# A two-layer graph network on one core: the first layer's gathered chunks as three-part 16-bit rows

## The reference, cut to what matters

```python
# 12500 nodes x 32 values; 212500 edges, sorted by dst
# layer 0: sum of scaled neighbour rows
norm = deg_inv_sqrt[row] * deg_inv_sqrt[col]
msgs = embedding_weight[row] * norm[:, None]
out = jax.ops.segment_sum(msgs, col, num_segments=n)
x = _layernorm(x + out, axis=-1)
# layer 1: an edge network makes 4 x 8 x 8 weights per edge, messages are summed by dst
x = _layernorm(x + _L1_gnn_ref(x, ...), axis=-1)
```

## Time and profile before

| | |
|---|---|
| median of 3 runs | 3307.98 us (3302.31 to 3311.62) |
| the profiled execution | 3305.82 us, its span 3304.0 us |
| layer 0's counted and gathered stage | from about 80 to 1182 us of the span |
| PE / DVE / ACT / POOL busy over the span | 79% / 87% / 38% / 72% |
| chain that ended last, by engine | POOL 31%, PE 22%, DVE 22%, issue 14%, ACT 10% |

### The profile page before, as it was taken

The page is one execution under the profiler, slowest core; times in us unless marked ns, Lnnn a source line. Parts: engine busy times, 40 slices in busy tenths (PEclk is TensorE's granted clock), DMA queues, the critical chain, the costliest instruction groups (busy, mean ns, idle before and its releaser), DMA issues.

```text
span 3304.0 us, 49643 instructions
## 1 busy us (share of the span) xinstructions
PE 2608.2 (79%) x17448; PEld 1564.6 (47%) x17534; DVE 2882.3 (87%) x5078; ACT 1267.8 (38%) x1963; POOL 2386.6 (72%) x2477
## 2 busy tenths in 40 slices
PE   5799999999989967777777777777777777777776
PEld 4567676766667743333333333333343333333333
DVE  7777877777777749999999999999999999999998
ACT  2787878887878741111111111111111111111111
POOL 1777777777767747777777777777777777777775
PEclk6899999999999988998888989988888888988897
DMA  3000000000000021111111111111111111111112
GB/s 79 13 14 14 14 14 14 14 13 14 14 13 14 14 35 32 28 28 28 28 28 28 28 32 29 28 28 28 28 28 29 31 28 29 28 28 28 28 32 37
DMA packets 169352, 84.63 MB, mean 26 GB/s; under 512 B 112473, under 2 KB 155289, under 8 KB 169113
## 3 DMA queue, kind: packets, MB, share of 16 engines
q0 software_dynamic: 78336, 40.26, 8.2%
q1 hardware_dynamic: 90777, 41.20, 5.3%
HBM read 76.48 MB, written 4.81 MB: 25 GB/s over the span
## 4 chain that ended last, share of the span: by engine, by line
POOL 31%; PE 22%; DVE 22%; issue 14%; ACT 10%; DMA 1%; DVEq 1%; POOLq 0%; SPq 0%; ACTq 0%
POOL xg L551 31%; PE ps L813 10%; ACT room L619 9%; DVE stage L1514 7%; PE ps L828 5%; DVE prod_all L1504 4%; PE ps L753 3%; DVE prod_all L1498 3%; DVE oh L1190 1%; DVE prod_all L1324 1%; DVE stage L1488 1%; PE ps L800 1%; DVE stage L1484 1%; PE ps L721 1%; DVE lane L1322 1%
## 5 line engine op out<-in xcount | busy, mean ns | idle before, releaser
L551 POOL DMA_INDIRECT xg<-x_table,idx x1664 | 1572.6, 945 | 545.4 <-issue 501.6
L551 POOL DMA_INDIRECT xg<-scaled_x_table,efT_all x784 | 801.4, 1022 | 285.7 <-issue 226.0
L619 ACT ACTIVATE room<-ps 128x1089 bf16<-128x1089 f32 x800 | 880.3, 1205 | 204.9 <-PE ps L813 204.5
L936 PE MATMUL ps<-w2t,hT 128*128 128x512 f32 x1664 | 883.7, 657 | 18.1 <-ACT hT L670 17.9
L1514 DVE TENSOR_REDUCE stage<-prod_all 128x192 f32<-128x1536 f32 x416 | 725.4, 1744 | 3.2
L813 PE MATMUL ps<-prod_all,lane 128*128 128x363 bf16 x2640 | 560.8, 321 | 111.1 <-ACT room L619 64.4
L936 PEld LDWEIGHTS ps<-w2t,hT 128*128 128x128 f32 x1664 | 346.7, 214 | 377.3 <-issue 248.0
L828 PE MATMUL ps<-stage,room 128*128 128x96 bf16 x7840 | 465.6, 207 | 0.0
L670 ACT ACTIVATE hT<-ps,b 128x512 f32<-128x512 f32 x208 | 142.9, 687 | 830.1 <-PE ps L924 830.0
L924 PE MATMUL ps<-efT_all,w 128*128 128x512 f32 x416 | 266.5, 727 | 244.6 <-DMA sh<-in_sh 244.2
L828 PEld LDWEIGHTS ps<-stage,room 128*128 128x128 bf16 x7840 | 418.5, 98 | 84.4 <-issue 1.7
(11 more groups left out here) (155 smaller groups left out, 1627.5 us busy)
## 6 DMA issues: line engine op xcount, KB each, us to landing
efT_all<-in_efT SPq DMA_DIRECT2D x104, 256.0 KB
xg<-x_table,idx POOLq DMA_INDIRECT x1664, 2.4
xg<-scaled_x_table,efT_all POOLq DMA_INDIRECT x784
sh<-in_sh SPq DMA_DIRECT2D x104, 32.0 KB
idx<-in_src SPq DMA_DIRECT2D x104, 8.0 KB, 1.6
scaled_x_table<-room SPq DMA_DIRECT2D x2, 784.0 KB, 3.4
x_table<-x_sb SPq DMA_DIRECT2D x7, 224.0 KB, 4.4
out_rows<-room SPq DMA_DIRECT2D x6, 224.0 KB
```

Source lines behind the costliest of these rows:

```text
L551: pool.indirect_dma_start(to, None, table, bass.IndirectOffsetOnAxis(ap=at, axis=0)).then_inc(landed, 16)
L619: act.activation(counts[u % 2][:, :, t * TWIN:(t + 1) * TWIN].rearrange("p (r h) w -> p r h w", r=RANGES), ps_ring[i % 2].rearrange("p r ( ...
L936: mm = pe.matmul(ps_bank[j % 2][v], hT[j // 2][:, t * P:(t + 1) * P], w2t[:].rearrange("p h c o i -> p (h c o i)"), start=False, stop=True)
```

## The change

From the third chunk on (n >= 2), a chunk's rows come from a second DRAM table, `split_d`, a copy of the three-part 16-bit table that SP writes once `low_part` is done. Each gather then brings 128 rows of 96 16-bit values (192 bytes for 128 before). The masks of these chunks are written as 16-bit values, PE sums them by 16-bit products with 96 stationary columns, and DVE adds 96 partitions in place of 32. The first two chunks stay as they were. The buffers move into one SBUF tensor, `gathered`, and share space; DVE's wait for the remapped indices moves ahead of the first chunk's masks, since their place now holds what the remapping reads. The other branch (graphs whose edges are not near) joins the parts on DVE and does not run here.

```diff
+        split_d = nc.dram_tensor("split_table", (NPAD, D3), BF16).ap()
...
-        xg = [sb(f"xg{k}", [P, TPC, D]) for k in range(2)]
+        SPLIT = TPC * D3 // 2
+        OH_AT = SPLIT + TPC * D
+        gathered = sb("gathered", [P, OH_AT + 2 * TPC * SW])
+        xg = [gathered[:, k * SPLIT:k * SPLIT + TPC * D].rearrange("p (t f) -> p t f", f=D) for k in range(2)]
+        xs = [gathered[:, k * SPLIT:(k + 1) * SPLIT].bitcast(BF16).rearrange("p (t f) -> p t f", f=D3) for k in range(2)]
...
+        oh_b = [gathered[:, at:at + TPC * SW // 2].bitcast(BF16).rearrange("p (t w) -> p t w", w=SW)
+                for at in (2 * SPLIT, OH_AT + TPC * SW)]
...
+        ps_sum3 = ps[0:D3, 7, 0:SPC * SW].rearrange("p (s w) -> p s w", s=SPC)
...
+            sp.wait_ge(s_low_part, 1)
+            sp.dma_start(split_d.rearrange("(l h) f -> l h f", l=P), table).then_inc(s_split, 16)
...
                 if n >= 2:
                     pool.wait_ge(s_sum[0], n - 1)
+                    pool.wait_ge(s_split, 16)
...
-                    gather_rows(xg[n % 2][:, t, :], y_d, idx0[:, n * TPC + t:n * TPC + t + 1], s_g[n % 2])
+                    gather_rows((xg if n < 2 else xs)[n % 2][:, t, :], y_d if n < 2 else split_d, idx0[:, n * TPC + t:n * TPC + t + 1], s_g[n % 2])
...
+                to, rows, ones = (ps_sum[0], xg[k], oh[0][k]) if n < 2 else (ps_sum3, xs[k], oh_b[k])
                 for t in range(TPC):
-                    mm = pe.matmul(ps_sum[0][:, t // TPS, :], xg[k][:, t, :], oh[0][k][:, t, :],
+                    mm = pe.matmul(to[:, t // TPS, :], rows[:, t, :], ones[:, t, :],
...
-                dve.tensor_tensor(oh[layer][k], rel_b[:, a:a + TPC].unsqueeze(2).to_broadcast([P, TPC, SW]),
+                dve.tensor_tensor(oh_b[k] if layer == 0 and n >= 2 else oh[layer][k], rel_b[:, a:a + TPC].unsqueeze(2).to_broadcast([P, TPC, SW]),
...
-                    dve.tensor_tensor(sumT_all[0:D, at], sumT_all[0:D, at], ps_sum[0][:, v, :],
+                    rows, of = (D, ps_sum[0]) if n < 2 else (D3, ps_sum3)
+                    dve.tensor_tensor(sumT_all[0:rows, at], sumT_all[0:rows, at], of[:, v, :],
...
                         if u == 0 and t == 4:
+                            dve.wait_ge(s_remap, 4)
                             one_hots(0, 0)
-                            dve.wait_ge(s_remap, 4)
                             one_hots(0, 1)
```

More of the change, by code:

```diff
@@ L222, in gnn_program @@
         idx0 = efT_all[:].rearrange("p k e -> p (k e)")[:, 0:CG * TPC].bitcast(I32)
-        oh_all = [sb(f"oh{k}", [P, TPC, SW]) for k in range(2)]
+        oh_all = [gathered[:, OH_AT + k * TPC * SW:OH_AT + (k + 1) * TPC * SW].rearrange("p (t w) -> p t w", w=SW)
+                  for k in range(2)]
+        oh_b = [gathered[:, at:at + TPC * SW // 2].bitcast(BF16).rearrange("p (t w) -> p t w", w=SW)
+                for at in (2 * SPLIT, OH_AT + TPC * SW)]
+        assert 2 * SPLIT + TPC * SW // 2 <= OH_AT + TPC * SW
         oh = [[o[:] for o in oh_all]] * 2
-        idx0_block = oh_all[1][:].rearrange("p t w -> p (t w)")[:, 0:CG * TPC].bitcast(I32)
+        idx0_block = oh_all[0][:].rearrange("p t w -> p (t w)")[:, 0:CG * TPC].bitcast(I32)
         stage = sb("stage", [P, NP * D3 // 2])
@@ L252, in gnn_program @@
         dst_c = key
-        high = oh_all[0][:].rearrange("p t w -> p (t w)")[:, 0:DT]
+        high = oh_all[1][:].rearrange("p t w -> p (t w)")[:, 0:DT]
         unit_first = sb("unit_first", [1, U], I32)
@@ L258, in gnn_program @@
         parts = sb("parts", [P, D])
-        ident_b = sb("ident_b", [P, P], BF16)
+        ident_b = lane_i[:, 0:P // 2].bitcast(BF16)
         flat = prod_all[:].rearrange("p b t c i o -> p (b t c i o)")
@@ L272, in gnn_program @@
         picked = flat1[:, 0:HB * D].rearrange("p (h f) -> p h f", f=D)
+        whole_rows = flat1[:, 1000:1000 + TPC * D].rearrange("p (t f) -> p t f", f=D)
         part_rows = flat1[:, 512:512 + HBS * D].rearrange("p (j f) -> p j f", f=D)
@@ L327, in gnn_program @@
         s_own = sem("s_own")
+        s_split = sem("s_split")
+        s_whole = sem("s_whole")
         s_remap = sem("s_remap")
@@ L856, in pick_rows @@
                 pe.wait_ge(s_ohs, tile * 2 + 3)
-                pe.matmul(ps_low, ohlow[:, 0, 0:P], ident_b[:], start=True, stop=True).then_inc(s_turned, 1)
+                pe.matmul(ps_low, ohlow[:, 0, 0:P], ident_b, start=True, stop=True).then_inc(s_turned, 1)
                 pe.wait_ge(s_turnedc, tile + 1)
@@ L886, in _ @@
                     wide_sums(0, xg[k], k, (s_g[k], 16 * TPC))
[L887 to L890, removed]
+                with pe.Fori(2, CG) as n:
+                    wide_sums(0, whole_rows, n, (s_whole, 2 * n - 2))
                 with pe.Fori(0, DT // TPC) as m:
@@ L1372, in clear_pads, with join_parts @@
                 dve.memset(counts[k][:, :, UT * TWIN:P], 0.0).then_inc(s_pads, 1)
+            def join_parts(n):
+                k = n % 2
+                dve.wait_ge(s_g[k], 16 * TPC * (n // 2 + 1))
+                dve.wait_ge(s_sum[0], n)
+                dve.tensor_tensor(whole_rows, xs[k][:, :, 2 * D:D3], xs[k][:, :, D:2 * D], ALU.add).then_inc(s_whole, 1)
+                dve.wait_ge(s_whole, 2 * n - 3)
+                dve.tensor_tensor(whole_rows, whole_rows, xs[k][:, :, 0:D], ALU.add).then_inc(s_whole, 1)
             def add_picked_rows(m, t):
@@ L1445, in _ @@
                 low_part()
-                dve.tensor_copy(ident_b[:], ident[:]).then_inc(s_ohs, 1)
+                dve.tensor_copy(ident_b, ident[:]).then_inc(s_ohs, 1)
                 dve.wait_ge(s_ohs, 1)
@@ L1455, in _ @@
                 dve.wait_ge(s_far, 3)
-                for c in range(CPP):
-                    add_wide_sums(0, c, of=(dst_f, c * TPC))
-                with dve.Fori(1, CG // CPP) as i:
-                    for c in range(CPP):
-                        add_wide_sums(0, i * CPP + c, of=(dst_f, i * PT + c * TPC))
-                for n in range(CG // CPP * CPP, CG):
+                for n in range(CG):
+                    if n >= 2:
+                        join_parts(n)
                     add_wide_sums(0, n, of=(dst_f, chunk_tile(n)))
```

## The result

The changed kernel takes **3287.18 us** (median of 6 runs, 3282.56 to 3289.57) against 3310.41 us of the kernel before in runs beside it: a ratio of 0.9935, 95% interval 0.9923 to 0.9946. The gain is 23 us, about half of the 42 us that were forecast; the time lies in the range. The profiled execution took 3286.85 us with a span of 3285.1 us, 18.9 us under the span before.

What follows compares the result with a forecast made beforehand. PE bounds layer 0, POOL right behind at 97% occupied. POOL's waits 26.3 us, the last sums' delay 14.6 and their shrinkage 1.53 give 42.4 off 3307.98: 3266 us; range 3244 to 3296, the forecast's own 3255 to 3275.

Steps and rivals of the forecast that it cites:

- What bounds: Layer 0: PE is the bound now, with POOL right behind it, 97% occupied by its own work.
- PE's products: PE's sums, chunks 2 to 48: 2.23 us falls to 0.70 a chunk, the weight load hidden; 71.9 us of PE's time.
- The wider gather: POOL's gathers in `gather_rows`: 945 ns unchanged at 192 bytes; rival: they cost more, 3443 to 3621 us, chance 0.10.
- the table's write: Split table's write before the third chunk's gathers: about 9 us, done near 103, 30 us of cover, cost 0.
- DVE: DVE's masks, adds and earlier wait on `s_remap` in layer 0: cost nothing, masks still at 1.41 us.
- POOL's 26.3 us of waits vanish: POOL's gathers, layer 0: with PE ahead its waits for PE go, last gather issued 26.3 us earlier, at 1131.7.
- The last sums can start there: End of layer 0: last sums start when their rows land, at 1134.1, no longer 14.6 us after landing.
- the rival on masks: Layer 0: faster 16-bit masks mean shorter blocking of gathers, 12 to 20 us more gain, 3246 to 3254; chance 0.14.
- The other 29.5 us become PE waiting: Layer 0: the 29.5 us of PE's gain that POOL leaves unused become PE's waits for gathers before its sums.
- Layer 1 the same: Layer 1: same instructions, only starting earlier by what layer 0 gains.
- PE losing its lead: PE in layer 0: its clock falls after waits for gathers, a smaller gain, 3275 to 3295 us; chance 0.15.
- no effect: Layer 0: supposed PE-bound time is POOL's pace, so waits only move from POOL to PE, 3298 to 3308; chance 0.08.

Runs made afterwards that it cites:

- later sums: Changed kernel with each chunk's sums, from the third chunk on, placed one turn later in PE's order: 3280.30 us, ratio 0.9902 to the kernel before.
- pairs and later sums: Changed kernel with masks written in pairs of tiles from the fourth chunk and sums one turn later from the third: 3257.25 us, ratio 0.9853.
- 15 rows: 15 of each chunk's 16 gathers: changed kernel 3234.22 us (0.9781), kernel before 3306.16 us (0.9986).
- pairs: Changed kernel with masks written in pairs of tiles from the fourth chunk on, PE reading them at a 4-byte stride: 3268.31 us, ratio 0.9880.

## Why the prediction was wrong in its size, and where it was right

- *What bounds.* Right: PE was the bound before (one gather fewer a chunk, or no masks, moved nothing by more than 0.14%) and POOL stood right behind it (after, one gather fewer moves 53 us).
- *PE's products.* Right: 0.70 us a chunk was forecast and measured, and the weight load hides, at a median of 125 ns. By the Trainium skill's rule (TensorE: Matmul & The Clock Gate, LDWEIGHTS (loading the stationary operand)) the text had 1.3 us as an estimate; the trace does not bear that out for 96 columns, and the measurement decides. The prediction took the row of 104 columns for half that load time, a misreading: it shows 122 ns at the least. The runs show loads of 125 ns by their own record, and yet a pair of load and product every 44 ns.
- *The wider gather, the table's write, DVE.* Right: 945 ns for 192 bytes; the third chunk's gathers start at 131.87 us, no later than before. DVE's masks keep 1.41 us, as the forecast had it against its rival.
- *"With PE ahead, POOL's 26.3 us of waits vanish."* They did, 25.3 us of them. **The step that failed is the next one, which took the rest of POOL's chain as fixed**: "its last gather is issued at 1158.0 - 26.3", that is at 1131.7. It was issued at 1141.60. The 761.0 us of busy time held 50 us in which DVE kept gathers waiting; the forecast knew of them (the rival on masks counts them) and left them in POOL's chain, but as an amount that stays. The busy time became 770.8 us, and the growth stands beside the masks, 24.5 to 34.5 us: in the trace, masks that begin just after a gather's start, at no more than 0.18 us each, fell from 23 to 5 of 46. The pair without masks shows that this time is now paid in full, 23 us, and that it cost nothing before. It was not that POOL stood waiting when a mask came: beside only 3 of the 46 masks before the change was its gap longer than the usual 0.30 us. The held time came back at later waits, which are 27 us longer without masks.
- *"The last sums can start there."* Mis-sized as well: they stand 4.9 us behind the landing, since PE's turn comes when its order says. With later sums PE reached the same turn 6.6 us before the rows, with as much half-clock time, so the place of the earlier sums in PE's order matters, and the clock alone does not explain the 4.9 us. Layer 1 then started 6.9 us earlier.
- *"The other 29.5 us become PE waiting."* Nearly right: 35.6 us in 11 waits. What the forecast had only among the rivals is the price of these waits, 58.1 us at 1.2 GHz against 13.6.
- *Layer 1 the same.* Right at the median (layer 1 starts 24.6 us earlier, the median falls by 23.2); its 5.7 us in the profile are within what this part varies by between profiles.
- *The rivals.* PE losing its lead gave 3275 to 3295, and the time lies there, but the mechanism carries at most the 5 to 7 us of the last sums: POOL's 45 waits on PE are all 0.3 us, its fixed gap, so a slow PE did not delay a gather in this trace. The half-clock time does go down with the time (35.3 us with pairs and later sums, 6.7 with 15 rows), but those edits act on the gathers, and the last gather moves by what they take from them. Shorter blocking did not come by the change; brought about with pairs it gave 19 us, where the rival had 12 to 20. That the measured time falls into the stated range, at 3287 of 3244 to 3296, is owed to the rival on PE's lead, which stretched that range, and not to the forecast's own sum, whose range ended at 3275. The wider gather and no effect are out.

## What to carry to other kernels

When two engines stand close together, relieving the first turns the second one's small stalls into the pace: holds that cost nothing, while a later wait gave the time back, are now paid in full. Nor do they keep their size, since what a hold costs depends on when it falls, and the change shifts that. So a busy time that contains holds belongs in a forecast as a range and not as a fixed number. A busy share does not show such an engine; its waits by releaser do, with the fixed gap behind each instruction taken off. And the cheapest test of which engine binds is to take one unit of work from it: 53 us after the change, 4 us before.

## What the runs showed of the hardware that was not expected

- A gather's time on POOL does not go by bytes: 945 ns in the median for 128 rows of 128 or of 192 bytes.
- The step between the moving columns of a 16-bit product has a price: sixteen products of 76 columns span 0.87 us contiguous, 0.88 at a step of 4 bytes, 2.39 at 32 bytes. Where between these two it begins was not tried.
- A gather that is issued while a mask runs (a DVE instruction with both operands in SBUF) ends 0.82 us after it: 2.11 us in all beside a mask of 1.41. A gather that began 0.13 us before the mask takes only 0.09 us more. The Trainium skill (SBUF — State Buffer, SBUF: two separate sides) describes an exclusive lock of ports that DVE and GpSimd share, held for a whole instruction by whichever starts first. The trace agrees with this for the gather that comes second; a mask that comes second is not held, it takes 1.42 us. The runs without masks price the masks at 23 us over 46 of them, in a kernel whose POOL has no slack. That four shorter masks hold as long as a long one was not expected, and nothing here says for certain why.
